# Expert layer: the last two shared tiles behind the routed tiles, scatters in two halves, and GpSimd's adding transfers ahead of the low parts

## What is computed

```python
xt = x.reshape(-1, 256)                        # layernorm(x), 4096 tokens
scores = softmax(xt @ gate_w.T)                # 8 experts
_, indices = top_k(scores + gate_bias, 2)      # two experts for each token
weights = take_along_axis(scores, indices)
mlp = lambda x, w1, w2, w3: (silu(x @ w1.T) * (x @ w3.T)) @ w2.T      # inner width 512
y = sum over e of mlp(xt, w1[e], w2[e], w3[e]) * combine[:, e:e + 1]  # routed part
out = x + tanh(g_ffn[1]) * (y + mlp(xt, sw1, sw2, sw3))               # and the shared expert
```

## Time and profile before

| | us |
|---|---|
| median of 3 runs | 3183.37 (3176.84 to 3183.44) |
| the profiled execution, its own time | 3195.05 |
| span of the profiled execution | 3193.4 |
| expert layer, from its first transpose to the span's end | 2648.4 to 3193.4 |
| busy over the span: PE / DVE / ACT / POOL | 93% / 69% / 57% / 40% |
| mean granted clock of TensorE, share of full speed | 0.97 |

### The profile page before, as it was taken

How to read it: one execution, slowest core, us unless ns; L and a number is a source line. 1 busy time by engine, 2 the same in 40 slices (tenths; PEclk the granted TensorE clock), 3 DMA queues, 4 the chain that set the end, 5 groups by cost and what they waited for, 6 DMA issues and landing times. The chain is left out here.

```text
span 3193.4 us, 48431 instructions
## 1 busy us (share of the span) xinstructions
PE 2961.9 (93%) x18056; PEld 2395.0 (75%) x18056; DVE 2218.2 (69%) x3785; ACT 1808.8 (57%) x2899; POOL 1266.6 (40%) x866
## 2 busy tenths in 40 slices
PE   5999999999999999999969958999999968999996
PEld 5888888788887888878859944555555438899996
DVE  6777777777777777776745547777777545478885
ACT  3555555555555555555535526888888843366664
POOL 2111111111111111111124427888887724468885
PEclk9999999999999999999979978999999988999998
DMA  8101010010100101000035644334433123268886
GB/s 263 38 11 34 11 37 11 17 34 11 37 11 17 34 11 37 11 16 21 5 113 202 213 122 134 106 120 120 119 115 100 41 80 113 86 180 237 232 231 170
DMA packets 201740, 279.23 MB, mean 87 GB/s; under 512 B 18035, under 2 KB 139538, under 8 KB 201456
## 3 DMA queue, kind: packets, MB, share of 16 engines
q1 hardware_dynamic: 182864, 245.48, 24.1%
q0 software_dynamic: 18656, 30.82, 5.0%
HBM read 194.50 MB, written 85.87 MB: 88 GB/s over the span
## 5 line engine op out<-in xcount | busy, mean ns | idle before, releaser
L309 POOL TENSOR_TENSOR a_w_stage<-a_w_stage,a_consts 128x256 f32<-128x256 f32 x64 | 39.5, 617 | 1231.7 <-PE a_scores L36 1196.4
L1673 POOL TENSOR_TENSOR c_pT_lo<-c_prob,c_pT_hi 128x1024 fp32r<-128x1024 f32 x192 | 456.2, 2383 | 113.5 <-ACT c_pT_hi L1756 109.4
L395 ACT ACTIVATE a_prob<-a_scores,a_neg_max 128x1024 f32<-128x1024 f32 x256 | 286.1, 1117 | 362.4 <-DVE a_neg_max L493 359.2
L493 DVE TENSOR_REDUCE a_neg_max<-a_scores 128x1 f32<-128x1024 f32 x256 | 310.1, 1211 | 109.9 <-PE a_scores L36 107.2
L388 ACT ACTIVATE a_pT_hi<-a_probT 128x512 fp32r<-128x512 f32 x512 | 279.1, 598 | 188.0 <-PE a_probT L732 187.9
L1868 DVE TENSOR_REDUCE c_neg_max<-c_max 128x2 f32<-128x1024 f32 x248 | 302.1, 1218 | 69.4 <-PE c_max L2101 68.3
L440 DVE TENSOR_TENSOR a_pT_lo<-a_probT,a_pT_hi 128x512 fp32r<-128x512 f32 x512 | 327.4, 681 | 20.8 <-ACT a_pT_hi L388 20.8
L1750 ACT ACTIVATE c_prob<-c_scores 128x1024 f32<-128x1024 f32 x256 | 261.0, 1020 | 70.7 <-PE c_scores L2112 66.6
L732 PE MATMUL a_probT<-k_ident,a_prob 128*128 128x128 f32 x2048 | 268.5, 273 | 17.5 <-DVE a_pT_lo L440 17.5
L732 PEld LDWEIGHTS a_probT<-k_ident,a_prob 128*128 128x128 f32 x2048 | 233.0, 140 | 43.2 <-issue 22.6
L34 PE MATMUL m_h<-m_rT_hi,m_w_hi 128*128 128x256 f32 x880 | 255.2, 290 | 3.4 <-DVE m_rT_lo L2588 1.9
(11 more groups left out here) (339 smaller groups left out, 8524.9 us busy)
## 6 DMA issues: line engine op xcount, KB each, us to landing
m_w_in<-L_ffn_w_in SPq DMA_DIRECT2D x117, 512.0 KB
e_w_in<-L_ffn_w_in SPq DMA_DIRECT2D x32, 1024.0 KB, 6.9
qk_dram<-c_stage SPq DMA_DIRECT2D x64, 256.0 KB
c_q_rows<-qk_dram SPq DMA_DIRECT2D x32, 512.0 KB, 5.0
c_k_rows<-qk_dram SPq DMA_DIRECT2D x32, 512.0 KB, 5.8
rows_in_dram<-a_blank SPq DMA_DIRECT2D x1, 10062.0 KB, 38.9
m_row_in<-rows_in_dram SPq DMA_DIRECT2D x39, 258.0 KB
a_w_stage<-L_xattn_Wq_in SPq DMA_DIRECT2D x64, 128.0 KB, 2.2
```

The source lines that it names most:

```text
L395: a(prob[:, qt, :], ps_s[:, qt % 2, :], ACT.Exp, bias=neg_max[:, qt:qt + 1], accum_out=row_sum[:, par, qt:qt + 1]).then_inc(exp_done, 1)
L493: ve.tensor_reduce(neg_max[:, qt:qt + 1], ps_s[:, qt % 2, :], AX.X, ALU.max, negate=True).then_inc(max_done, 1)
L1673: g.tensor_tensor(flat(pT[1][:, kt - 1]), flat(prob[:, kt]), flat(pT[0][:, kt - 1]).bitcast(F32), ALU.subtract).then_inc(lo_pool, 1)
```

## The change

The last two of the 16 shared tiles move behind the 39 routed ones: NA = 14, routed tiles are n = 14 to 52, FIRST = 53 and LAST = 54 are shared tiles 14 and 15, with the shared weights loaded a second time as number 40. Their residual rows are stored into `sums` at the beginning, fetched back (`back`) when all adds have landed, and the two results go from `acc` straight to the output, by ScalarE's queue. The other 14 tiles are copied from `sums` in seven transfers of half the size. The scatter is spread over 12 tiles, with two semaphores and two writes of the second weight, one for each half of the tokens. In routed tile n, GpSimd issues `add(n-2)` ahead of the two `low` of tile n+1, not behind them. TensorE makes `second_product` of tiles 51 and 52 in a row, within tile 52.

```diff
-        NA = B * S // R1
+        NS = B * S // R1
+        NA = NS - 2
+        HALF = NT // 2
...
+        FIRST = NA + NR
+        LAST = NS + NR - 1
...
         def number(n):
-            return max(n - NA + 1, 0)
+            return min(max(n - NA + 1, 0), NR + 1)
 
         def routed(n):
-            return n >= NA
+            return NA <= n < FIRST
...
             dma(blank_v, z[:, 0:RT, 0:D]).then_inc(kept, 16)
+            for j in range(NA, NS):
+                dma(sums_v[:, j], acc[:, RT * j:RT * j + RT]).then_inc(kept, 16)
...
-            sp.wait_ge(scattered, 16 * TOP * NT)
+            for half in range(2):
+                sp.wait_ge(scattered[half], 16 * TOP * HALF)
...
-            for n in range(NA + 3, LAST + 1):
+            for n in range(NA + 3, FIRST):
                 bring(n)
+            sp.wait_ge(w_lo, 2 * NR - 2)
+            for j in range(2):
+                load(0, j, shared_views[j])
+            sp.wait_ge(w2_lo, NR)
+            load(0, 2, shared_views[2])
             sp.wait_ge(summed, 16 * RT * NR)
-            for i in range(0, B * S, B * S // 4):
-                part = slice(i, i + B * S // 4)
+            for j in range(NA, NS):
+                dma(acc[:, RT * j:RT * j + RT], sums_v[:, j]).then_inc(back, 16)
+            for i in range(0, NA * R1, S):
+                part = slice(i, i + S)
                 dma(out_rows[part].rearrange("(p r) d -> p (r d)", p=P), sums[part].rearrange("(p r) d -> p (r d)", p=P)).then_inc(out_stored, 16)
...
-            for n, count in enumerate((4, 4, 4, 5, 5, 5, 5)):
+            for n, count in enumerate((5, 5, 5, 5, 6, 6)):
                 pool.wait_ge(t_full, n + 1)
...
-            pool.wait_ge(second_weight, 1)
             first = 0
-            for n, count in enumerate((5, 5, 5, 5, 4, 4, 4)):
-                pool.wait_ge(t_full, n + 8)
+            for n, count in enumerate((5, 5, 6, 5, 5, 6)):
+                pool.wait_ge(t_full, n + 7)
+                pool.wait_ge(second_weight, 1 if n < 3 else 2)
...
-            for n in range(NA, LAST + 1):
-                if n < LAST:
-                    low(number(n + 1), 0)
-                    low(number(n + 1), 1)
+            for n in range(NA, FIRST):
                 if n >= NA + 2:
                     add(n - 2)
-            add(LAST - 1)
-            add(LAST)
+                low(number(n + 1), 0)
+                low(number(n + 1), 1)
+            add(FIRST - 2)
+            add(FIRST - 1)
...
+            for n in (FIRST, LAST):
+                act.wait_ge(o_out, n + 1)
+                j = n - NR
+                nc.scalar.dma_start(out_rows[R1 * j:R1 * j + R1].rearrange("(t p) d -> p t d", p=P), acc[:, tokens(n)]).then_inc(last_stored, 16)
+            act.wait_ge(last_stored, 32)
...
-                if n:
+                if n and n not in (FIRST, LAST):
                     result(n - 1)
-                if n == 7:
-
-                    dve.wait_ge(scattered, 16 * NT)
-                    ve.tensor_copy(z[:, :, D + 1:D + 2].rearrange("p t o -> p (t o)"), weight[:]).then_inc(second_weight, 1)
+                if n == FIRST - 1:
+                    result(n)
+                if n in (4, 6):
+
+                    half = n // 6
+                    part = slice(HALF * half, HALF * half + HALF)
+                    dve.wait_ge(scattered[half], 16 * HALF)
+                    ve.tensor_copy(z[:, part, D + 1:D + 2].rearrange("p t o -> p (t o)"), weight[:, part]).then_inc(second_weight, 1)
+            dve.wait_ge(back, 32)
+            result(FIRST)
             result(LAST)
...
-                if n:
+                if n and n != FIRST:
                     second_product(n - 1)
+                if n == FIRST - 1:
+                    second_product(n)
             second_product(LAST)
```

More of the change, by code:

```diff
@@ L2392, in layer1_experts @@
         o_full, o_out = sem("o_full"), sem("o_out")
-        kept, summed, out_stored = sem("kept"), sem("summed"), sem("out_stored")
-        LAST = NA + NR - 1
+        kept, summed, back, out_stored, last_stored = (sem(n) for n in ("kept", "summed", "back", "out_stored", "last_stored"))
+        FIRST = NA + NR
+        LAST = NS + NR - 1
         views = [v.rearrange("e (c p) f -> p e c f", p=P) for v in (w1_d, w3_d, w2_d)]
@@ L2398, in layer1_experts @@
         sums_v = sums[0:B * S].rearrange("(j t p) d -> p j t d", t=RT, p=P)
+        shared_views = ffn.shared_views
         blank_v = sums[B * S:].rearrange("(t p) d -> p t d", p=P)
         out_rows = out_dram.rearrange("b s d -> (b s) d")
-        assert NA % 2 == 0
+        assert NA % 2 == 0 and NR % 2 == 1 and LAST == FIRST + 1
         def number(n):
-            return max(n - NA + 1, 0)
+            return min(max(n - NA + 1, 0), NR + 1)
         def routed(n):
-            return n >= NA
+            return NA <= n < FIRST
         def tokens(n):
-            return slice(RT * n, RT * n + RT)
+            j = n if n < NA else n - NR
+            return slice(RT * j, RT * j + RT)
         def product(n, f):
@@ L2517, in _ @@
                 first += count
-                if n in (4, 5):
-                    low(1, n - 4)
-            for n in range(NA, LAST + 1):
-                if n < LAST:
-                    low(number(n + 1), 0)
-                    low(number(n + 1), 1)
+                if n in (3, 4):
+                    low(1, n - 3)
+            for n in range(NA, FIRST):
                 if n >= NA + 2:
                     add(n - 2)
-            add(LAST - 1)
-            add(LAST)
+                low(number(n + 1), 0)
+                low(number(n + 1), 1)
+            add(FIRST - 2)
+            add(FIRST - 1)
         @block.scalar
@@ L2561, in _ @@
                 m = number(n)
-                ahead = routed(n) and n < LAST
-                if ahead:
+                if routed(n):
                     split(m + 1, 0)
@@ L2576, in _ @@
                 hidden_high(n, 3)
-                if routed(n):
+                if routed(n) or n == FIRST:
                     split_w2(m)
```

11 lines of the change are left out of this document (6 added, 5 removed).

## The result

| | us |
|---|---|
| kernel before, on the same chip | 3183.4 (3176.84 to 3183.63, 4 runs) |
| changed kernel | **3288.5** (3286.06 to 3292.31, 4 runs) |
| ratio | 1.0336, 95% interval 1.0320 to 1.0351 |
| profiled execution of the changed kernel | 3286.06, span 3284.4 |

The change makes the kernel 105 us slower. The forecast was 3230, +47, with 3260 as its upper end: the direction was right, the size was less than half of what came, and the time lies outside the range.

The account below looks back on a forecast made before the run. TensorE's matmuls were taken to bound the routed stage before, at 9.10 us a tile, and a GpSimd-VectorE loop after. Profiled 3195.05 + 67 - 17 - 13 = 3232; from timed 3183.4, 3220 or 3233; taken 3230, range 3197 to 3260.

Parts of the forecast that it names:

- part 1: Routed tiles: adds ahead of low parts on GpSimd close a loop through held VectorE; +67 us over 37 tiles.
- The loop of 10.9 us: Routed tile: adds and low parts 8.51, hidden_low 0.29, w2_low 1.15, result 0.87, lag 0.1; 10.9 us against 9.10.
- if it doesn't slip in, 11.3: Routed tile: if hidden_low(n, 2) doesn't get between the low parts, 0.35 us more, 11.3 a tile, +81 in all.
- The clock, a rival with 0.05: Routed stage: TensorE idles 1.9 us a tile, clock falls to 1.2 GHz in one tile of five; 3290 us, chance 0.05.
- just comes ahead of the w1 low part: Routed tile: VectorE's hidden_low(n, 1) was taken to run before GpSimd's w1 low part; a step of the 10.9 us loop.
- a granted clock under 1.00 in the routed stage: Routed stage: a sign that would show the forecast wrong.
- Part 2: End of kernel: shared tiles last leave 32 us behind the last low part against 49.3; -17 us.
- Part 3: Head: scatter in halves removes a TensorE loss beside 15 unbroken scatters; -13 us of the profiled span, perhaps absent in timed runs.
- no burst over 8 us: Head: a sign of being right, no burst of scatters on GpSimd over 8 us and no issue gaps.
- VectorE isn't held: Routed stage rival: VectorE not held, or wins the race; 9.35 us a tile, 3162 or 3175 us, chance 0.10.
- the loop closes over two tiles: Routed stage rival: w2_low gets ahead of the low part, 10.0 us a tile; 3186 or 3200 us, chance 0.08.
- The prediction's row for a product that is not held: VectorE, routed tile before the change: product with one input in PSUM, 0.41 us from 3006.51, read as not held.

Follow-up runs that it names:

- the run with filled stands: Changed kernel with 16 extra matmuls per routed tile, 10 and 6 ahead of TensorE's two waits for low parts: 3261.4 us, ratio 1.0250 to the kernel before.
- the result ahead and the wait: Changed kernel with result(n-1) ahead of w2_low(n) on VectorE and GpSimd's low parts waiting for hidden_low(n, 1): 3237.0 us against 3196.0 of before, ratio 1.0122.
- the run with the gap: Changed kernel with GpSimd waiting for hidden_low(n, 2) between the two low parts: 3287.0 us, ratio 1.0329 to the kernel before.

## Why the prediction was wrong, step by step

- **Direction and loop of part 1: right.** The loop "adds, low parts, held VectorE, result, adds" is there, released by m_res; TensorE waits for m_w_lo; the order alone costs what the kernel lost.
- **The loop of 10.9 us: too short, by 0.6.** Uniform tiles take 11.5 at full clock. The adds and low parts take 8.19, not 8.51 (-0.3). The lag between the result's end and the add was taken as 0.1, from ScalarE's end to a low part's start; an adding transfer starts 0.77 after what releases it (3009.16 + 0.87 = 3010.03, then 3010.80): +0.67. That is another kind of instruction, and the price of the nearest row was not the price. And `hidden_low(n, 2)` does not slip in between the low parts: +0.3 (2.55 us from the last low part to the result's end, where the prediction had 0.29 + 1.15 + 0.87 = 2.31). The prediction had this as a condition ("if it doesn't slip in, 11.3"). In the trace of before the low parts had 0.24 or 0.27 us between them only because ScalarE's high part came late; behind the adds both are ready, and there is no gap. 37 x 0.6 = 22 us.
- **The clock, a rival with 0.05: this was the larger miss.** It was weighed as one stand of 1.9 us in 11 and priced as matmuls at half speed. The stand is 3.1 to 3.4 us in two pieces in about every second tile, since TensorE waits for each of the two low parts; the clock falls behind nearly each of these; and the price is not the slow matmuls, which the slack of the loop would hide, but that `hidden_low(n, 1)` arrives 1 us after the low parts instead of ahead of them. The prediction had said "just comes ahead of the w1 low part" without asking what moves it. The 18 long tiles bring 454.15 - 37 x 11.5 = 29 us more, 1.6 each. That this rival's number, 3290, lies beside the measured time is luck: it is 8 tiles at 7 us of slow matmuls, and there were 18 at 1.6. The prediction's own sign of being wrong, a granted clock under 1.00 in the routed stage, did come.
- **Part 2, -17 us: the end came where it was forecast**, L + 32.8 against L + 31 to 33, with the last result later (L + 25.7 against L + 23.3). In the runs all the other parts together bring 14 us with the low parts first and 10 with the adds first.
- **Part 3: 0 in the timed runs, as the text took for likelier.** On a chip with the stall the halves give 15 us, where -13 was forecast. The sign "no burst over 8 us" did not come: in the changed kernel's first tiles 15 scatters run together, 19.7 us from 2652.8, without a stall like that one.
- **The sum.** 3183.4 + 67 - 17 = 3233, taken as 3230. With 22 and 29 more it is 3284; measured 3288.5. No run places the 4 us that are left.

The rivals "VectorE isn't held" and "the loop closes over two tiles" did not come. The first has no support in any run: instructions with two inputs in SBUF are held in every one of them. The prediction's row for a product that is not held (3006.51) stands beside an adding transfer and not beside a low part; in the run with filled stands one of 0.42 us at 3002.76 does run unheld beside the low part from 3002.73. The second did not come even with the result put ahead of w2's low part (10.3 to 10.9).

## What to carry to other kernels

When an engine's order is changed so that two instructions which were kept apart by a late input become adjacent, whoever is locked out by them can be locked out for both: look at why the gap was there. Here it was so wherever GpSimd came from the adds to both low parts without a wait. Where a step "just" comes ahead of another, compute what happens when it comes 1 us later, at TensorE's lower clock too, since a loop with a race in it can lose it again and again (18 tiles of 37 here). Work that nobody waits for, as these adds, belongs behind the work that somebody waits for; of this change the version with the low parts first, the two shared tiles last and the halved scatter is the best of all (0.9953 and 0.9912 of before).

## What the runs showed of the hardware

- **A held VectorE instruction can be locked out through two GpSimd instructions.** Where GpSimd came from the adds to both low parts without a wait, the pair takes 5.2 to 5.3 us, the second record starts 0.6 us before the first ends, and the VectorE instruction was held to the end of the second: 6.12 us for one of 1.22. Where GpSimd had waited in front of the pair, it takes 4.9 us, the second record starts as a rule 0.02 to 0.05 us before the first ends, and VectorE got in between (30 of 34 tiles with the result ahead and the wait). With a gap of 1 us between them it got in every time. What makes the difference between the first two is not shown. The Trainium skill, "SBUF — State Buffer", section "Who interferes with whom", says that whoever issues first has the shared ports for the whole instruction and the other is blocked; the trace agrees for one instruction, and by that alone the VectorE instruction, which waited since the first, would have been due before the second. It was in the tiles of the second kind and was not in those of the first.
- **How far ahead a VectorE instruction must start is not read from the starts alone.** One that starts 0.75 us ahead of the low part's record costs nothing (3012.94, 0.42 us); one that starts 0.57 us ahead was held to its end (3001.62, 3.83 us, in the run with the gap).
- **GpSimd's indirect transfers start late behind a semaphore**: 0.77 us from the result's end to the record's start, 0.76 to 0.80 in every run in which the result releases the add (3007.75 + 0.87 = 3008.62 to 3009.38 with the result ahead and the wait), against 0.09 for a low part.
- **The clock's fall does not follow from the length of the stand alone**: it fell to 1.2 GHz after stands of 2.16 and 0.97 us (2992, 2994) and of 0.73 and 1.27 us (3028, 3030), and not after 2.15 and 1.25 us (3016, 3018). With 16 small matmuls in the stands it stays at 1.00 from 2900 to 3100.
- **The same kernel takes 3181 on some chips and 3195 on others.** On the one chip of the 3195 kind on which both were profiled, the traces differ by one stall of 13 us, and splitting the burst takes the kernel to 3180.
